# Layer norms inside attention and mixture of experts: moments by the aggregating instruction, the mean taken off by ScalarE

## The reference

```python
x = x + norm(attention(norm(x)))      # 16 heads of 16, causal softmax, projections wq, wk, wv, wo with biases
x = x + norm(experts(norm(x)))
# experts: the first token of each sequence picks 2 of 8 experts by x[:, 0] @ Wr + br;
#   for each of the two: gelu(x @ W1[e] + b1[e]) @ W2[e] + b2[e]; their mean
```

## Time and profile before

| | |
|---|---|
| median of 3 runs | 2214.8 us (2208.49 to 2218.28) |
| the profiled execution | 2213.8 us, of which the span of the profile is 2211.8 |
| PE busy over the span | 2042.2 us (92%) |
| DVE busy | 1844.0 us (83%) |
| ACT busy | 1343.4 us (61%) |
| POOL busy | 252.1 us (11%) |

### The profile page before, as it was taken

How to read it: one execution, slowest core, us unless ns; L and a number is a source line. 1 busy time by engine, 2 the same in 40 slices (tenths; PEclk the granted TensorE clock), 3 DMA queues, 4 the chain that set the end, 5 groups by cost and what they waited for, 6 DMA issues and landing times.

```text
span 2211.8 us, 39573 instructions
## 1 busy us (share of the span) xinstructions
PE 2042.2 (92%) x15696; PEld 850.2 (38%) x15696; DVE 1844.0 (83%) x3611; ACT 1343.4 (61%) x1637; POOL 252.1 (11%) x349
## 2 busy tenths in 40 slices
PE   6997699999999999999999999999999997799997
PEld 3664123333333333333333333333333323566664
DVE  6885798989998988889898898989898963899983
ACT  3664166677777677777767667767766674233332
POOL 4000011100101011010101110010101102322000
PEclk9999599999999999999999999999999998999999
DMA  3999800313214040421403041231404004554320
GB/s 109 284 282 236 177 11 15 83 38 67 63 35 93 7 92 21 85 50 48 90 11 92 18 80 38 66 68 33 92 6 93 12 22 125 139 138 114 92 70 30
DMA packets 169098, 178.25 MB, mean 81 GB/s; under 512 B 20178, under 2 KB 143314, under 8 KB 168914
## 3 DMA queue, kind: packets, MB, share of 16 engines
q1 hardware_dynamic: 162002, 163.12, 29.9%
q0 software_dynamic: 6912, 12.61, 2.6%
HBM read 107.76 MB, written 67.63 MB: 79 GB/s over the span
## 4 chain that ended last, share of the span: by engine, by line
PE 56%; DVE 21%; ACT 7%; issue 3%; SPq 1%; DMA 1%; POOL 0%; ACTq 0%; DVEq 0%; POOLq 0%
PE b_psO L942 20%; PE b_psS L924 15%; DVE b_pmax L820 13%; PE b_ring L896 12%; ACT b_prob L861 5%; PE c_psH L1294 3%; PE b_ring L893 3%; PE c_psO L1307 2%; PE c_psA L1264 1%; DVE c_attn L103 1%; DVE c_ln_x_stats L79 1%; DVE c_ln_f_stats L79 1%; DVE c_x L1137 1%; DVE c_ffn L1185 1%; DVE c_y L103 1%
## 5 line engine op out<-in xcount | busy, mean ns | idle before, releaser
L820 DVE TENSOR_REDUCE b_pmax<-b_ring 128x1 f32<-128x512 f32 (+4 forms) x2336 | 1377.2, 647 | 178.2 <-PE b_ring L896 172.9
L861 ACT ACTIVATE b_prob<-b_psS 128x1024 f32<-128x1024 f32 (+3 forms) x1280 | 1082.7, 896 | 455.5 <-PE b_psS L924 451.1
L924 PE MATMUL b_psS<-g_qT,g_kT 64*128 64x512 bf16 (+7 forms) x5120 | 752.0, 347 | 19.4 <-ACT b_prob L861 12.8
L896 PE MATMUL b_ring<-g_kT,g_qT 64*128 64x512 bf16 (+3 forms) x2560 | 700.0, 354 | 12.1 <-DVE b_pmax L820 7.7
L942 PE MATMUL b_psO<-b_prob,g_v 128*32 128x512 f32 (+3 forms) x5120 | 601.0, 542 | 1.2 <-POOL b_prob L806 0.3
L924 PEld LDWEIGHTS b_psS<-g_qT,g_kT 64*128 64x128 bf16 (+1 forms) x5120 | 289.1, 94 | 217.0 <-ACT b_prob L861 92.3
L896 PEld LDWEIGHTS b_ring<-g_kT,g_qT 64*128 64x128 bf16 x2560 | 201.1, 95 | 437.6 <-DVE b_pmax L820 362.0
L806 POOL TENSOR_SCALAR_AFFINE_SELECT b_prob<-b_prob 128x512 f32<-128x512 f32 x256 | 163.1, 637 | 1660.0 <-ACT b_prob L861 1660.0
L893 PE MATMUL b_ring<-later,query_of 64*128 64x128 bf16 x1024 | 179.6, 225 | 49.0 <-PEq L284 33.2
L893 PEld LDWEIGHTS b_ring<-later,query_of 64*128 64x128 bf16 x1024 | 79.0, 94 | 257.4 <-DVE b_pmax L820 200.0
L942 PEld LDWEIGHTS b_psO<-b_prob,g_v 128*32 128x32 f32 x5120 | 101.9, 108 | 171.9 <-issue 151.5
(11 more groups left out here) (96 smaller groups left out, 1003.6 us busy)
## 6 DMA issues: line engine op xcount, KB each, us to landing
qk_parts<-a_parts SPq DMA_DIRECT2D x64, 384.0 KB, 4.5
g_qT<-qk_parts SPq DMA_DIRECT2D x192, 128.0 KB, 4.3
g_kT<-qk_parts SPq DMA_DIRECT2D x192, 128.0 KB, 4.3
v_ones<-a_v SPq DMA_DIRECT2D x64, 256.0 KB, 4.1
g_v<-v_ones SPq DMA_DIRECT2D x32, 512.0 KB, 5.8
out_sums<-b_outT SPq DMA_DIRECT2D x64, 256.0 KB, 2.9
a_x<-in_L_attn_x SPq DMA_DIRECT2D x16, 512.0 KB, 4.9
c_x<-in_L_attn_x SPq DMA_DIRECT2D x16, 512.0 KB, 7.8
```

What stands on the lines that cost most here:

```text
L820: nc.vector.tensor_reduce(pmax[:, c % 2].rearrange("p (h t) n -> p h t n", t=TT)[:, heads[0]:heads[-1] + 1:2, qt, pc], ring[:, bank, 0:k * ...
L861: nc.scalar.activation(prob[:, j % PBUF, 2 * s:2 * s + 2, off:CH], psS[:, 2 * s:2 * s + 2, off:CH], ACT.Exp).then_inc(exp_done, 1)
L896: ins_ = nc.tensor.matmul(ring[:, bank, i * w:(i + 1) * w], qT[own, g, h // 2, 0, t * P:(t + 1) * P], kT[own, g, h // 2, 0, pc * CH:pc * C ...
L924: ins_ = nc.tensor.matmul(psS[:, 2 * s + p, off:CH], kT[own, g, s, ab, kt * P:(kt + 1) * P], qT[own, g, s, ab, c * CH + off:(c + 1) * CH], ...
```

## The change

In all four norms the six small ops behind bn_stats are replaced by bn_aggr, one for each token, which gives mean and variance as a pair. In the attention and ffn norms of stage C, VectorE negates the mean, ScalarE adds the negated mean to the chunk in place (`centre`: four Identity activations with a bias per partition), and VectorE then scales by the inverse root and adds x or x1 in one instruction for each token (`scale_and_add`); the separate full-width adds are gone. The tail of `experts_end` becomes `add_experts`, which stands behind `take_projection` in VectorE's order. In the norms in front (stage A, and x1 to y) `normalise` stays as it was.

```diff
-LN_MARKS = 4
+LN_MARKS = 2
     def variance(self, chain, src, var_done):
         for t in range(TT):
-            last = v.bn_stats(st[:, t, :], src[:, t])
+            last = v.bn_stats(self.stats[:, t, :], src[:, t])
         chain.mark(last)
         chain.wait()
-        v.tensor_tensor(tmp[:, 0, :], st[:, :, 1], st[:, :, 4], ALU.subtract)
-        v.tensor_tensor(tmp[:, 1, :], st[:, :, 2], st[:, :, 5], ALU.add)
-        chain.mark(v.tensor_tensor(tmp[:, 2, :], st[:, :, 1], st[:, :, 4], ALU.add))
-        chain.wait()
-        v.scalar_tensor_tensor(out=tmp[:, 3, :], in0=tmp[:, 0, :], scalar=float(D // 4), in1=tmp[:, 0, :],
-                               op0=ALU.mult, op1=ALU.mult)
-        chain.mark(v.tensor_scalar(self.mean[:, :], tmp[:, 2, :], 0.5, None, ALU.mult))
-        chain.wait()
-        v.tensor_tensor(self.var[:, :], tmp[:, 3, :], tmp[:, 1, :], ALU.add).then_inc(var_done, 1)
+        for t in range(TT):
+            last = v.bn_aggr(self.moments[:, t, :], self.stats[:, t, :])
+        last.then_inc(var_done, 1)
+
+    def negate_mean(self, v, var_done, count, less_done):
+        v.wait_ge(var_done, count)
+        self.nc.vector.tensor_scalar(self.less[:, :], self.moments[:, :, 0], -1.0, None, ALU.mult
+                                     ).then_inc(less_done, 1)
+
+    def centre(self, tokens):
+        for t in range(TT):
+            last = self.nc.scalar.activation(tokens[:, t], tokens[:, t], ACT.Identity, bias=self.less[:, t:t + 1])
+        return last
+
+    def scale_and_add(self, chain, centred, other, dst):
+        self.invert(chain)
+        for t in range(TT):
+            last = self.nc.vector.scalar_tensor_tensor(out=dst[:, t], in0=centred[:, t], scalar=self.rstd[:, t:t + 1],
+                                                       in1=other[:, t], op0=ALU.mult, op1=ALU.add)
+        return last
...
                 ln_a.variance(Chain(v, chain_a, n * LN_MARKS), attn, var_a)
+                ln_a.negate_mean(v, var_a, n + 1, less_a)

             def add_attention(b, c, n):
                 v.wait_ge(std_a, n + 1)
-                ln_a.normalise(Chain(v, chain_a, n * LN_MARKS + LN_MARKS - 1), attn, attn).then_inc(norm_a, 1)
-                v.wait_ge(norm_a, n + 1)
+                v.wait_ge(centred_a, n + 1)
                 v.wait_ge(x_ld[c % 2], (b * 2 + c // 2 + 1) * 16)
-                nc.vector.tensor_tensor(x1[:, c], x_sb[:, c % 2], attn[:, :, :], ALU.add).then_inc(x1_done, 1)
+                ln_a.scale_and_add(Chain(v, chain_a, n * LN_MARKS + LN_MARKS - 1), attn, x_sb[:, c % 2], x1[:, c]
+                                   ).then_inc(x1_done, 1)
...
-                ln_f.variance(chain, ffn, var_f)
+                ln_f.variance(Chain(v, chain_f, n * LN_MARKS), ffn, var_f)
+                ln_f.negate_mean(v, var_f, n + 1, less_f)
+
+            def add_experts(b, c, n):
+                p = c % 2
                 v.wait_ge(std_f, n + 1)
-                ln_f.normalise(chain, ffn, ffn).then_inc(norm_f, 1)
-                v.wait_ge(norm_f, n + 1)
+                v.wait_ge(centred_f, n + 1)
                 v.wait_ge(stored[p], 16 + (b * 2 + c // 2) * 16)
-                nc.vector.tensor_tensor(out_sb[:, p], x1[:, c], ffn[:, :, :], ALU.add).then_inc(out_done, 1)
+                ln_f.scale_and_add(Chain(v, chain_f, n * LN_MARKS + LN_MARKS - 1), ffn, x1[:, c], out_sb[:, p]
+                                   ).then_inc(out_done, 1)
...
-                                (4, take_projection), (2, route)):
+                                (4, take_projection), (0, add_experts), (2, route)):
...
             def root_attn(b, c, n):
                 act.wait_ge(var_a, n + 1)
                 ln_a.root(consts.eps, std_a)
+                act.wait_ge(less_a, n + 1)
+                ln_a.centre(attn).then_inc(centred_a, 1)

             def root_ffn(b, c, n):
                 act.wait_ge(var_f, n + 1)
                 ln_f.root(consts.eps, std_f)
+                act.wait_ge(less_f, n + 1)
+                ln_f.centre(ffn).then_inc(centred_f, 1)
```

More of the change, by code:

```diff
@@ L68, in __init__ @@
         self.stats = sb(name + "_stats", [P, TT, 6], F32)
-        self.tmp = sb(name + "_tmp", [P, 4, TT], F32)
-        self.mean = sb(name + "_mean", [P, TT], F32)
-        self.var = sb(name + "_var", [P, TT], F32)
+        self.moments = sb(name + "_moments", [P, TT, 2], F32)
+        self.less = sb(name + "_less", [P, TT], F32)
         self.std = sb(name + "_std", [P, TT], F32)
@@ L75, in variance @@
     def variance(self, chain, src, var_done):
[L77 removed]
+        v = self.nc.vector
         for t in range(TT):
[L79 removed]
+            last = v.bn_stats(self.stats[:, t, :], src[:, t])
         chain.mark(last)
         chain.wait()
[L82 to L84 removed]
@@ L85, in variance @@
-        chain.wait()
-        v.scalar_tensor_tensor(out=tmp[:, 3, :], in0=tmp[:, 0, :], scalar=float(D // 4), in1=tmp[:, 0, :],
-                               op0=ALU.mult, op1=ALU.mult)
-        chain.mark(v.tensor_scalar(self.mean[:, :], tmp[:, 2, :], 0.5, None, ALU.mult))
-        chain.wait()
-        v.tensor_tensor(self.var[:, :], tmp[:, 3, :], tmp[:, 1, :], ALU.add).then_inc(var_done, 1)
-    def root(self, eps, std_done):
-        self.nc.scalar.activation(self.std[:, :], self.var[:, :], ACT.Sqrt, bias=eps[:, 0:1],
-                                  scale=1.0 / D).then_inc(std_done, 1)
+        for t in range(TT):
+            last = v.bn_aggr(self.moments[:, t, :], self.stats[:, t, :])
@@ new lines, in variance, with root @@
+        last.then_inc(var_done, 1)
[3 more added lines that the diff above has]
+                                     ).then_inc(less_done, 1)
+    def root(self, eps, std_done):
+        self.nc.scalar.activation(self.std[:, :], self.moments[:, :, 1], ACT.Sqrt, bias=eps[:, 0:1]
+                                  ).then_inc(std_done, 1)
+    def centre(self, tokens):
+        for t in range(TT):
+            last = self.nc.scalar.activation(tokens[:, t], tokens[:, t], ACT.Identity, bias=self.less[:, t:t + 1])
+        return last
@@ L97, in normalise, with invert @@
+    def invert(self, chain):
+        chain.mark(self.nc.vector.reciprocal(self.rstd[:, :], self.std[:, :]))
+        chain.wait()
     def normalise(self, chain, src, dst):
-        v = self.nc.vector
-        chain.mark(v.reciprocal(self.rstd[:, :], self.std[:, :]))
-        chain.wait()
+        self.invert(chain)
         for t in range(TT):
-            last = v.tensor_scalar(dst[:, t], src[:, t], self.mean[:, t:t + 1], self.rstd[:, t:t + 1],
-                                   ALU.subtract, ALU.mult)
+            last = self.nc.vector.tensor_scalar(dst[:, t], src[:, t], self.moments[:, t, 0:1], self.rstd[:, t:t + 1],
+                                                ALU.subtract, ALU.mult)
+        return last
@@ L1008, in stage_c @@
         std_a, std_x, std_f = sem("c_std_a"), sem("c_std_x"), sem("c_std_f")
-        norm_a = sem("c_norm_a")
+        less_a, less_f = sem("c_less_a"), sem("c_less_f")
+        centred_a, centred_f = sem("c_centred_a"), sem("c_centred_f")
         x1_done = sem("c_x1_done")
```

3 lines of the change are left out of this document (removed).

## The result

The changed kernel takes 2219.8 us (median of 20 runs, 2212.5 to 2224.8) against 2214.2 us before (20 runs, 2207.8 to 2218.8): ratio 1.0023, 95% interval 1.0012 to 1.0034. It is about 5 us slower, less than the 0.5% that counted as a change. The prediction was 2218 us.

A forecast was written before the change was run, and what follows sets the result against it. Stage C was taken as bound by TensorE's 18.1 us step, beside a nearly equal ScalarE and VectorE loop. Terms -0.6, -4.0, +3.5 and +4.2 gave +3.1 on 2213.8, 2216.9, with the median 1.0 above: 2218 us, range 2202 to 2234.

The forecast's parts named there:

- the filling: Stage C's pipeline start, up to the first `outer`, bound by VectorE in order: 4.0 us shorter.
- the twelve steps: Stage C from the first `outer` to that of chunk 12: 235.8 us before, forecast to change by -0.6 us.
- the last three: Stage C's final steps, with no projection beside them: +3.5 us of TensorE waits and +4.2 us of slower clock.
- the stalls that are left: VectorE's scalings still held by GpSimd's product in stage C: two of 2.1 us, 4.2 us together.
- the fall of the clock: TensorE slowed after long waits at stage C's end: 2.6 us each at four chances in five, +4.2 us.
- a longer loop: Stage C's ScalarE and VectorE loop grows 1.18 us; less 0.4 us slack, an undisturbed step goes from 18.1 to 18.9.
- swallowed stalls: VectorE's wait before the attention norm grows from 1.4 to 5 us, taking in the router's ops and most GpSimd collisions.
- the 1899: Sign in the profile after: the first `outer` of stage C starts near 1899 us; before it was 1903.31.
- The rival of 0.20 apart: In the norms, aggregates don't overlap, so each norm loses its 0.38 us gain: +13 us, 2231 us; chance 0.22.
- The rival of a cheap centring: On ScalarE in stage C, centring activations come 0.24 us apart and TensorE stays the bound: 2201 us; chance 0.12.
- the meetings: In stage C, GpSimd's product for `cc` collides with VectorE's ops, mostly 2 us stalls, some ten in the trace before.
- That rival: Stage A starts earlier, its scalings passing between GpSimd's two memsets: -6.8 us, 2211 us; chance 0.12.

The follow-up runs named there:

- centre_late: The changed kernel with ScalarE's centring of ffn moved from right after root_ffn to after the first two gelus of the next step: ratio to before 0.9943.
- copy_first: The changed kernel with copy_y placed in front of root_ffn in ScalarE's order: ratio to before 0.9971.
- second profile: The changed kernel run once more as it was, to profile another execution: ratio to before 1.0020.
- small_after: The changed kernel with GpSimd's product for cc cut to 2 columns of 1024: ratio to before 0.9974, and 0.9983 when run again.
- small_before: The kernel before with GpSimd's product for cc cut to 2 columns of 1024: ratio to before 0.9920.
- vector_centre_copy: The changed kernel with VectorE centring attention before the root, ffn normalised and added on VectorE, copy_y before root_ffn: 2192.1 us, ratio to before 0.9894.
- attn_only: The changed kernel with the ffn norm put back to normalise and add on VectorE, attention still centred on ScalarE: ratio to before 0.9919.
- aggr_only: The kernel before with only bn_aggr put in for the small ops in all four norms: ratio to before 0.9912.

## Why the prediction was right

**The sum.** The changed kernel's profiled execution took 2215.4 us, 1.6 above that of before, where 3.1 were forecast: -2.4 ahead of the first `project` (nothing forecast; this varies between executions), -2.4 in the filling (-4.0), -0.1 in the twelve steps (-0.6), +6.2 in the last three (+7.7), +0.2 at the end (0). It is 4.5 below the median of the changed kernel. That the time came within 2 us of 2218 is partly luck: the step was taken too short, and the stalls that are left, the filling's gain and the fall of the clock too large, as the parts below show. The mechanism, a longer loop against swallowed stalls, is what the runs show. Also by luck the first `outer` started at 1898.5, near the 1899 that was named as a sign: half of that came ahead of stage C.

**The bound.** Shown. With nothing removed, only placed elsewhere, the undisturbed step went from 19.31 to 18.10 (centre_late) and 18.43 (copy_first). VectorE's 57 us less of work shortened nothing, where busy shares alone would have promised a gain.

**Aggregates.** Four take 0.38 us, so 0.08 apart as taken (0.38 less 0.157, over three): the root starts 0.46 us after the end of the last bn_stats, at 0.47 taken and 0.85 with the six ops. The rival of 0.20 apart is refuted.

**Centring.** Taken at 0.49 each and 0.39 apart, measured 0.496 and 1.62 us until the copy is issued (1.56 taken); the wait in attention grew by 1.65 (1.56 taken). The Trainium skill's page ScalarE: Activation LUTs, section What ACT_TABLE_LOAD costs, gives 280 ns and 0.833 ns for each element of an activation with a pointer bias, by which I estimate 493 ns for 256 elements, and an overlap of 93 ns between successive ones; the trace agrees with the first to 3 ns (493 and 496 ns), and four that follow each other took 1.69 to 1.71 us, so 0.09 of overlap each. The rival of a cheap centring is refuted.

**The scaling with add** was mis-sized: I took 426 ns from a row with a constant as its scalar; with a scalar for each partition it is 480, and four take 1.67 us, 0.21 more than taken. That it is the scalar that makes the difference is read from these two rows and was not tested by itself. With 0.09 and 0.06 more for the two centrings it makes 0.36 of the 0.43 by which the undisturbed step is longer than my sum (19.31 for 18.88); the other 0.07 fit a slack of 0.33 in place of the 0.4 taken.

**Swallowed stalls.** The mechanism is shown: the twelve steps lose 12.2 us without the meetings (222.0 to 234.2) and -0.1 or 3.4 with them (235.8 to 235.7 or 239.2), and the timed loss is 12 us without and 5 with them. Timelines of GpSimd and VectorE in the changed kernel:

```profile
1922.39 2.35 POOL L1131 TENSOR_TENSOR c_cc<-c_cc,c_inv 128x1024 f32<-128x1024 f32 x1 [6.15 <-DMA c_inv<-inverse_sums]
...
2037.11 2.35 POOL L1131 TENSOR_TENSOR c_cc<-c_cc,c_inv 128x1024 f32<-128x1024 f32 x1 [5.24 <-DMA c_inv<-inverse_sums]
...
1923.71 2.51 DVE L119 SCALAR_TENSOR_TENSOR c_x<-c_attn,c_ln_a_rstd,c_x 128x256 f32<-128x256 f32 x4
...
2037.55 1.92 DVE L1176 SCALAR_TENSOR_TENSOR c_rt<-c_rt,c_best,place 1x8 f32<-1x8 f32 x1
```

The first meeting cost 0.84 us on the loop; the second stalls a 1x8 op of the router by 1.7 us inside VectorE's idle time and costs nothing. In that profile only two meetings reach the scalings, 1.5 us where I took 4.2, plus no clock fall (1.5 taken) and no weight wait (0.5 taken). They stand in the first two steps, after 11.0 and 8.6 us from the issue of the loads to the product; in all later steps that took 7.5 to 8.4 us, and at the later batch boundaries the loads of 11 us and more, on which my two stalls rested, didn't come. So the twelve steps came to 235.7 against 235.2 taken, by luck, by two errors against each other: 12 x 0.4 too little in the undisturbed step, too much in the rest. In the second profile they are 239.2.

**The filling.** -2.4 us against -4.0 taken. (The terms that I gave for one round add up to -1.6, not to -1.4.) TensorE there waited 2.45 us for the experts' weights, which were issued 5.7 us earlier than before but landed later after their issue; the filling was 48.8 us in one profile of small_after and 44.5 in the other, so this term was finer than it could be.

**The last three steps.** +6.2 against 3.5 + 4.2 = 7.7: 61.6 in place of 55.4. The waits grew by 3.9 us (3.5 taken: 5.19, 3.77 and 3.75 us, before 3.74, 2.57 and 2.55). The clock fell in all three, as expected, but the eight matmuls took 5.3 to 5.4 us and not 6.3, also in the first, where before they had taken 6.3: +2.4 where 4.2 was taken.

**Stage A.** That rival fell as argued against it. GpSimd's and VectorE's timelines at the start of the changed kernel:

```profile
5.47 13.93 POOL L276 MEMSET g_kT<- 1x8192 bf16 x2
...
6.59 0.38 DVE L83 BATCH_NORM_AGGREGATE a_ln_moments<-a_ln_stats 128x2 f32<-128x6 f32 x4
...
7.54 12.65 DVE L111 TENSOR_SCALAR a_xn<-a_x,a_ln_moments,a_ln_rstd 128x256 f32<-128x256 f32 x4
```

The four aggregates pass beside the memset at 6.59, and the scalings then stand from 7.54 until the second memset is done; 12.65 us for 1.38 of work. xn is ready at 20.2, 0.4 us sooner than before. The Trainium skill's SBUF — State Buffer, section Who interferes with whom, says that a VectorE instruction with at most one SBUF input, outside the two-port modes, doesn't contend with GpSimd, and that `tensor_scalar` can enter such a mode and then does. The trace agrees if the aggregate (0.38 us for four beside the memset) is of the first kind and the scaling, a `tensor_scalar`, of the second.

## What to carry to other kernels

Before moving work to an engine with idle time, follow the loop that the pipeline closes through all engines, and see in whose order the work will stand: four activations of 0.5 us in front of a copy cost 1.6 us in each step, while the same four a few instructions later cost nothing in an undisturbed step. An idle time in front of an instruction may be shelter: here it hid the router and most collisions with GpSimd, and taking it away brought little. A change of several parts can hide a good one: the aggregates alone made the kernel 0.9% faster, and the centring of ffn took all of it back.

## What the runs showed that I had not expected

- A late TensorE often pays twice. After a wait of 3.07 us the next eight matmuls took 6.64 us in place of 3.70, after 3.77 us 5.39, after 2.0 us and less in no profile more than 3.70. The wait alone doesn't settle it: after 2.55 us they took 3.70 in the kernel before and 5.37 in small_before, after 2.13 us 5.37 in vector_centre_copy, and after 3.58 us 5.40 in centre_late but 3.70 in attn_only:

```profile
2142.37 3.70 PE L1314 MATMUL c_psH<-c_yT,c_w1e 128*128 128x512 f32 x8 [3.58 <-ACT c_hT L1244]
```

- Over the 20 runs of the changed kernel the time goes with the mean granted clock of the whole execution: 0.974 at 2212.5 us, 0.969 at 2224.8. In which stage the clock fell is known for the profiled ones alone, and there stage B accounts for most of the difference. That kernels in which TensorE waits less also differ less from run to run is not shown: vector_centre_copy took 2191.7 to 2193.6 in four runs, but aggr_copy 2186.8 to 2198.9 in six.
- One profile can miss a cost that the runs have: the first profile of the changed kernel showed a meeting at 0.84 us, the second the same meeting at 5 us, with what followed on TensorE. The timed difference between the kernel and its cut form (11 us the first time) told it first.
- A two-input instruction on 8 numbers of one partition is held by GpSimd's product just as a full-width one (1.92 us for 0.22 of work).
